# First attention layer of a four-layer graph network: biases of queries and keys as columns at the eviction instead of products with ones

## What is computed

```
q = h @ Wq + bq;  k = h @ Wk + bk;  v = h @ Wv + bv          # layer 0, 12 heads of 32
scores = q k^T / sqrt(32) + beta * adj;  masked where adj is not over 0
x = x + softmax(scores) v
x = x + directed(h; W_left, W_self, W_right, biases)          # layer 1, one pass
x = x + directed(directed(h))                                 # layer 2, two passes
x = x + attention(h; Wq, Wk, Wv, bv, adj as bias) @ Wo.T + bo # layer 3: no bias on q and k
```

## Time and profile before

| what | value |
|---|---|
| median of three runs | 2525.0 us |
| profiled execution: its own time | 2528.0 us |
| profiled execution: span of the core | 2526.3 us |
| mean granted TensorE clock | 0.972 of full speed |
| TensorE busy | 2353.9 us (93%) |
| VectorE busy | 1981.3 us (78%) |
| ScalarE busy | 1778.4 us (70%) |
| GpSimd busy | 1635.4 us (65%) |
| chain that ended last, by engine | TensorE 82%, GpSimd 3%, DMA 2% |

### The profile page before, as it was taken

How to read it: one execution, slowest core, us unless ns; L and a number is a source line. 1 busy time by engine, 2 the same in 40 slices (tenths; PEclk the granted TensorE clock), 3 DMA queues, 4 the chain that set the end, 5 groups by cost and what they waited for, 6 DMA issues and landing times.

```text
span 2526.3 us, 80379 instructions
## 1 busy us (share of the span) xinstructions
PE 2353.9 (93%) x26817; PEld 1741.8 (69%) x26817; DVE 1981.3 (78%) x8945; ACT 1778.4 (70%) x4412; POOL 1635.4 (65%) x2196
## 2 busy tenths in 40 slices
PE   2259999999999999999999999999999999999985
PEld 1146777777777777777777777777777777777753
DVE  4557788888887878888878888878888888888873
ACT  2336777777777777777777777777777777777763
POOL 1026777677766766777677767766777677767762
PEclk8579999999999999999999999999999999999996
DMA  3311333233223332223232323232322223322321
GB/s 102 105 51 39 69 66 70 60 72 63 69 62 66 65 71 58 67 65 73 58 66 65 74 59 68 65 68 62 64 66 71 62 64 66 71 62 64 63 53 35
DMA packets 479851, 165.39 MB, mean 65 GB/s; under 512 B 413392, under 2 KB 479440, under 8 KB 479440
## 3 DMA queue, kind: packets, MB, share of 16 engines
q1 hardware_dynamic: 479440, 160.25, 28.6%
HBM read 46.92 MB, written 12.58 MB: 24 GB/s over the span
## 4 chain that ended last, share of the span: by engine, by line
PE 82%; POOL 3%; issue 3%; DMA 2%; DVE 1%; ACT 0%; SPq 0%; DVEq 0%; POOLq 0%; ACTq 0%
PE bank L148 20%; PE bank L150 20%; PE bank L149 20%; PE bank L1360 4%; PE bank L1298 4%; PE bank L1347 2%; DMA pT<-p 2%; PE bank L1252 1%; PE bank L1314 1%; PE bank L1316 1%; PE bank L1315 1%; PE bank L1405 1%; PE bank L1403 1%; PE bank L1402 1%; POOL p L587 1%
## 5 line engine op out<-in xcount | busy, mean ns | idle before, releaser
L148 PE MATMUL bank<-w_hi,dir_hT_hi 128*128 128x384 f16 x1728 | 564.7, 327 | 0.0
L149 PE MATMUL bank<-w_lo,dir_hT_hi 128*128 128x384 f16 x1728 | 564.3, 327 | 0.0
L150 PE MATMUL bank<-w_hi,dir_hT_lo 128*128 128x384 f16 x1728 | 564.1, 326 | 0.0
L587 POOL TENSOR_TENSOR p<-probs,p 128x512 f16<-128x512 f32 x384 | 447.1, 1164 | 133.8 <-ACT p L699 133.1
L692 ACT ACTIVATE probs<-minus_scores,minus_max 128x128 f32<-128x128 f32 x1536 | 488.1, 394 | 63.1 <-DVE minus_max L909 63.1
L148 PE MATMUL bank<-hT_hi,w_hi 128*128 128x128 f16 x2304 | 412.6, 220 | 0.7 <-DVE hT_lo L895 0.7
L149 PE MATMUL bank<-hT_lo,w_hi 128*128 128x128 f16 x2304 | 412.5, 220 | 0.0
L150 PE MATMUL bank<-hT_hi,w_lo 128*128 128x128 f16 x2304 | 412.4, 220 | 0.0
L909 DVE CUSTOM_DVE_ANT_0 minus_scores<-bank,minus_score_bias 128x128 f32<-128x128 f32 x1536 | 343.5, 286 | 23.7 <-issue 13.4
L595 POOL TENSOR_TENSOR raw_weights<-raw_weights,gain_offset 128x384 f32<-128x384 f32 x192 | 191.9, 999 | 166.4 <-ACT raw_weights L779 166.4
L149 PEld LDWEIGHTS bank<-w_lo,dir_hT_hi 128*128 128x128 f16 x1728 | 169.5, 98 | 112.5 <-issue 1.2
(11 more groups left out here) (164 smaller groups left out, 7250.0 us busy)
## 6 DMA issues: line engine op xcount, KB each, us to landing
x<-in_x SPq DMA_DIRECT2D x64, 192.0 KB, 2.6
dir_adj_tile<-in_adj SPq DMA_DIRECT2D x192, 64.0 KB, 2.1
out<-raw_weights SPq DMA_DIRECT2D x64, 192.0 KB, 2.2
adj_tile<-in_adj SPq DMA_DIRECT2D x128, 64.0 KB, 2.1
pT<-p SPq DMA_TRANSPOSE x384, 2.8
raw_weights<-in_L_gnn_Wq SPq DMA_DIRECT2D x2, 576.0 KB, 4.2
raw_weights<-in_L_gnn_Wk SPq DMA_DIRECT2D x2, 576.0 KB, 5.6
raw_weights<-in_L_gnn_Wv SPq DMA_DIRECT2D x2, 576.0 KB, 6.4
```

The source lines that it names most:

```text
L148: pe.matmul(out, stat[0], move[0], start=first, stop=False)
L149: pe.matmul(out, stat[0], move[1], start=False, stop=False)
L150: return pe.matmul(out, stat[1], move[0], start=False, stop=last)
L587: pool.tensor_tensor(p16[:, c, 1, :, :], probs[:, HC * c:HC * c + HC, :], p16[:, c, 0, :, :], ALU.subtract).then_inc(p_lo[c], 1)
```

## The change

The bias products are taken out of `project_turned`. The q and k biases are loaded as columns, one value per partition, in six small DMAs ahead of the weights; GpSimd makes the scaled negative of the q bias once. The evictions of "first" tasks become three instructions of 128x128 each, with the column of their block as bias; those of "last" tasks stay. The two biases no longer take part in the search for the scales, and their rows are no longer made.

```diff
+        raw_columns, q_bias = sb("raw_q_k_bias_columns", [P, 2, C]), sb("minus_q_bias", [P, C])
+        columns_loaded = sem("q_k_bias_columns_loaded")
...
-        W0 = Weights(names("L0", "Wq", "Wk", "Wv"), names("L0", "bq", "bk"), [([0], [0]), ([1], [1]), ([2], [])], False,
-                     0, 0, 0, 2, 1, [(v_bias[:, :], ins["L0_gnn_bv"]), (raw_beta[:, :], ins["L0_gnn_beta"])])
+        W0 = Weights(names("L0", "Wq", "Wk", "Wv"), [], [([0], []), ([1], []), ([2], [])], False,
+                     0, 0, 0, 0, 2, [(v_bias[:, :], ins["L0_gnn_bv"]), (raw_beta[:, :], ins["L0_gnn_beta"])])
...
+                def load_columns(sp):
+                    for n, name in enumerate(("L0_gnn_bq", "L0_gnn_bk")):
+                        for c in range(C):
+                            sp.dma_start(raw_columns[:, n, c:c + 1], ins[name][c128(c)].rearrange("(p o) -> p o", o=1)).then_inc(columns_loaded, 16)
...
                 load_x(Task(ATTENTION, "first", 0))
+                load_columns(sp)
                 W0.load(sp)
...
                     pool.tensor_scalar(minus_beta[:, :], raw_beta[:, :], -1.0, None, ALU.mult).then_inc(w_kept_by_pool, 1)
+                    pool.wait_ge(columns_loaded, 32 * C)
+                    pool.tensor_scalar(q_bias[:, :], raw_columns[:, 0], -float(HD ** -0.5), None, ALU.mult).then_inc(w_kept_by_pool, 1)
...
-                    n = is_last(t)
-                    act.activation(qT[:, :], q_bank[:, 0:D], ACT.Copy, scale=q_unscale[:, n:n + 1]).then_inc(q_ready, 1)
+                    if is_last(t):
+                        act.activation(qT[:, :], q_bank[:, 0:D], ACT.Copy, scale=q_unscale[:, 1:2]).then_inc(q_ready, 1)
+                        return
+                    for c in range(C):
+                        part = act.activation(qT[:, c128(c)], q_bank[:, c128(c)], ACT.Identity, bias=q_bias[:, c:c + 1],
+                                              scale=q_unscale[:, 0:1])
+                    part.then_inc(q_ready, 1)
...
-                    act.activation(kT[:, :], k_bank[:, 0:D], ACT.Copy, scale=unscale[:, n:n + 1]).then_inc(k_ready, 1)
+                    if is_last(t):
+                        act.activation(kT[:, :], k_bank[:, 0:D], ACT.Copy, scale=unscale[:, n:n + 1]).then_inc(k_ready, 1)
+                        return
+                    for c in range(C):
+                        part = act.activation(kT[:, c128(c)], k_bank[:, c128(c)], ACT.Identity, bias=raw_columns[:, 1, c:c + 1],
+                                              scale=unscale[:, n:n + 1])
+                    part.then_inc(k_ready, 1)
...
-                W0.bias_rows_high(act, bias_rows, [(0, 0, 0), (1, 1, 1)])
                 W0.split_high(act)
...
-                W0.bias_rows_low(dve, bias_rows, [(0, 0, 0), (1, 1, 1)])
                 W0.split_low(dve)
...
                     for m in range(C):
-                        if not is_last(t):
-                            pe.matmul(bank[:, c128(m)], bias_rows[:, w, c128(m)], first_and_33rd[:, :], start=True, stop=False)
                         for c in range(C):
                             mm = three_products(pe, bank[:, c128(m)],
                                                 (weights.w_hi[:, w, c, c128(m)], weights.w_lo[:, w, c, c128(m)]),
-                                                hTs(t, c), first=c == 0 and is_last(t), last=c == C - 1)
+                                                hTs(t, c), first=c == 0, last=c == C - 1)
```

## The result

The changed kernel takes 2505.2 us (median of six runs, 2504.0 to 2508.0) beside 2524.9 us of the kernel before in the same series (six runs, 2523.4 to 2525.5). The ratio is 0.9924, interval 0.9911 to 0.9937: 19.7 us less. Forecast were 2504.3 us, in a range of 2499 to 2510. The profiled execution took 2505.8 us around a span of 2504.0, 22.3 less than the span before.

The account below looks back on a forecast made before the run. TensorE's back-to-back instructions were taken as the bound. Products -21.2 us, evictions nothing and start +0.5 made -20.7: 2528.0 profiled becomes 2507.3, and 3.0 less for the median gives 2504.3 us, range 2499 to 2510.

Parts of the forecast that it names:

- The bound: Middle rounds: TensorE's instructions one behind the other set the pace, 35.96 us for an undisturbed round.
- the six products: First layer's key and query projections, three bias products each: 0.056 us apiece, 0.336 us a graph, 21.2 us over 63 graphs.
- a pair costs more than its pitch: Rival at TensorE's bias products: the 98 ns weight load sets the spacing, so 37 us go, 2488 us; chance 0.03.
- The evictions: First-layer query and key evictions on ScalarE: each 0.6 us longer, 77 us more over 64 graphs, costing nothing in time.
- the cover: Three idle times on ScalarE hide the longer evictions; without it each graph would pay up to 1.2 us.
- 1.38 us of slack, of which 0.6 goes: Between the query eviction's end at 1233.86 and the scores' start at 1235.24; the longer eviction takes 0.6.
- ScalarE becomes the bound: Rival at the query eviction: over 1.38 us late at the scores, +54 us, 2579 us; chance 0.04.
- Transposed probabilities: Rival before the last third of first-layer heads: TensorE's waits take gain back, 3.4 us lost, 2507.7, or 2515; chance 0.08.
- The first graph: Left out of the saving: its longer evictions before the scores eat what the removed products save, so zero.
- The start: Loads, scale search and GpSimd chain before the first round: 0.9 - 1.0 + 0.6 = +0.5 us, bounds -3.5 and +3.5.
- The sum: Whole kernel: -21.2 + 0.5 = -20.7 us, giving 2507.3 us profiled and 2504.3 us as median.
- The rival of no change: A chain once per round without slack takes exactly the removed products' place, so the time stays; chance 0.05.

Follow-up runs that it names:

- The zero products: Changed kernel with six products per graph done again on TensorE with rows of zeros, columns staying on ScalarE: 2523.2 us, ratio 0.9989.
- The six-piece kernel: Changed kernel with query and key evictions of first tasks each cut into six instructions of 128x64 instead of three of 128x128: 2551.7 us, ratio 1.0100.
- the experiment with six pieces of queries: Changed kernel with only the query eviction of first tasks in six instructions of 128x64, the key's staying in three: 2515.8 us, ratio 0.9963.
- both edits: Changed kernel with negations of beta and query bias on VectorE and column loads issued behind the weights: 2501.1 us in second batch, 2497.4 in third.
- the columns behind: Changed kernel with the six column loads issued after the first layer's weights instead of ahead of them: 2501.7 us, ratio 0.9906.

## Why the prediction was right

**The bound and the six products: right.** The period fell by 0.33 us, forecast 0.336, to 35.63, forecast 35.62. The zero products alone bring 0.33 back. The rival by which a pair costs more than its pitch falls with this: removing six pairs from each round moved the period by 0.055 us each. For the 81 ns of the Trainium skill, "TensorE: Matmul & The Clock Gate", section "Back-to-back issue gap", cited in the prediction, this means that the trace did not agree, nor did the runs; 81 would have shown as 0.49 us a round.

**The evictions: right in size and in cost, wrong in the cover.** Each took 0.57 us more, forecast 0.6, one piece 453 to 468 ns, forecast 0.43 to 0.49. ScalarE rose by 70 us, forecast 77, to 74%. The idle time before the queries' eviction went to zero, as worked out. That before the exponent shrank from 0.61 to 0.31 only, where I had said to about zero: the queries' eviction ends 0.57 us later against the scores, but the exponent's operand from VectorE comes later too (0.50 us ahead of the scores instead of 0.77), and the difference of 0.30 is what the idle time lost. The left eviction behind it starts 0.16 us after the scores, 0.17 before, so nothing was handed on. The step that was mis-sized is "1.38 us of slack, of which 0.6 goes": the end of the eviction and the start of the scores are not neighbours at distance zero, for 0.25 us of hand-off belong between them. The real cover was 1.13 before and is 0.56 now. This changed nothing for the forecast, as 0.6 fits in 1.13, but it decides how near the edge the kernel stands: the experiment with six pieces of queries cost 11 us where I had forecast 0 to 5 by the same mistake. The condition of the rival "ScalarE becomes the bound", 1.38 us late, was for the same reason 0.25 too generous. The six-piece kernel shows that rival's mechanism, at 47.4 us, when it is forced.

**Transposed probabilities: right.** They are waited for 8 times and 4.5 us in all (10 and 6.7 before). Not one round in the median lost its gain.

**The first graph: the gain of half a microsecond is not the change's.** I took this graph as zero, because "its longer evictions eat what it saves". From the first product to the scores it is 5.90 us, before 6.40 (34.61 to 41.01). Timeline of TensorE after:

```profile
34.00 0.29 PE L148 MATMUL bank<-hT_hi,w_hi 128*128 128x128 f16 x1 [1.17 <-DVE hT_lo L915]
34.29 0.31 PE L148 MATMUL bank<-hT_hi,w_hi 128*128 128x128 f16 x1
...
37.10 0.22 PE L148 MATMUL bank<-hT_hi,w_hi 128*128 128x128 f16 x1
37.27 0.22 PE L148 MATMUL bank<-hT_hi,w_hi 128*128 128x128 f16 x1
...
39.90 0.95 PE L1315 MATMUL bank<-kT,qT 32*128 32x128 f32 x24 [1.29 <-issue]
```

The products start 0.107 us apart up to 37.05 and 0.056 after it: a slow stretch of 3.0 us from the first product on. In the kernel before it lasts 4.6 us (to 39.17), and in the two other profiled executions of the changed kernel 3.8 and 2.6, so its length moves without any edit. From the first product to the last it is 4.38 us, before 5.46 (34.61 to 40.07), so 1.08 less. 1.5 us less of the slow stretch is worth 0.7 of that by the two spacings, an estimate that leaves some 0.36 for the six products. Two kernels of the first batch show it without an estimate, since the slow stretch lasts 3.81 us in both: the repeated changed kernel and the one with the products back. First and last product of the repeated changed kernel:

```profile
34.19 0.29 PE L148 MATMUL bank<-hT_hi,w_hi 128*128 128x128 f16 x1 [1.18 <-DVE hT_lo L915]
...
38.95 0.22 PE L150 MATMUL bank<-hT_hi,w_lo 128*128 128x128 f16 x1
```

And with the products back:

```profile
33.77 0.29 PE L1279 MATMUL bank<-ones_in_rows_and,bias_rows 128*128 128x128 f16 x1 [1.18 <-DVE hT_lo L916]
...
38.86 0.22 PE L150 MATMUL bank<-hT_hi,w_lo 128*128 128x128 f16 x1
```

4.76 against 5.09 us: the six products are worth 0.33 us in the first graph too, and the longer query eviction costs 0.58 there (1.52 us from the last product to the scores, before 0.94). So the change itself makes the first graph some 0.25 us longer. My zero is near to this, and the half microsecond that the profile shows beside it is chance. The slow stretch is also what the first scores of the start's experiments lost: with the negations on VectorE the slow stretch lasts 4.6 us, with both edits 4.0 in the third batch and in the second until the last product.

The slow stretch looks like the lower level of the clock, which the views do not show: they give a granted clock of 1.00 on both sides of 37.05. But the trace's first record of the clock begins at 37.0 here, at 39.2 in the kernel before and at 38.0 in the repeated changed kernel, just where the spacing changes, and for the time ahead of it there is none. And in the stretch of 1691.20 to 1694.60 above, at a granted clock of 0.50, products of 128x128 start 0.107 us apart as well. TensorE had been idle until the transpositions (31.95) 2 us before the first product.

**The start: wrong in sign, small in size.** Forecast +0.5, bounds -3.5 to +3.5; measured -0.6 at VectorE's first work (-1.1 at the first scores, by the first graph's chance). VectorE's search began 0.4 later, not 0.9: six column loads cost 2.8 us of issue (1.36 + 1.38 for twice three), not 3.2. GpSimd was mis-sized more, in two terms of opposite sign. I left the first negation at its 1.21 us and added 0.6; it took 0.26, and the second 0.23, so two instructions took 0.57 us with the gap between them, where one had taken 1.21. And I took the idle stretch ahead of them as fixed; it went from 7.06 to 7.60 us, and with that ate the half microsecond by which the reduction ended earlier. None of this could be read off the old trace, and the bounds held it. At graph 5 the changed kernel is 0.5 us ahead, not 1.1: the wait of the weights' preparation for a transfer is 1.0 longer (20.3 us, 19.3 before). That wait was 21.5 and 19.6 us in other executions of changed kernels; it moves by 1 to 2 us for reasons that the edits do not explain.

**The sum: right, and in part by luck.** 20.7 us were forecast; the medians of the series differ by 19.7, and 22.3 came off the profiled span. The 58 rounds from graph 5 on gave 19.1, against 58 x 0.336 = 19.5 in the forecast. The five other graphs that I counted, four ahead of graph 5 and the last one, were to give 1.7 more, and no trace shows it. From the first graph's instruction on GpSimd to that of graph 5 it is 267.8 us before and 267.9 after (266.8 and 268.8 in the other two profiled executions of the changed kernel), so 1.3 us would be hidden in what that stretch moves by itself. And the end, with the last graph's projections in it, takes 131.0 us, 130.9 before. The start, forecast 0.5 later and come 0.6 earlier, made up for most of this. The 2.7 us by which the stalls of the two profiled executions differ are chance too: the round of 39.49 us with its fall of the clock alone is 3.5. It fits that this execution of the kernel before stood 3 us above its median, and that the spans differ by more than the medians. The rival of no change had a place to hold, a chain once per round without slack; there was none.

**Open.** What sets GpSimd's idle stretch after the reduction over partitions: 7.06 us before, 7.60, 7.59 and 7.18 in the changed kernel, 9.90 with the columns behind, 8.34 and 8.24 with both edits. Whether the order of the two waits matters in the changed kernel itself, where the slack of 0.56 should hide it, wasn't tried alone; the kernel without key bias has the other order and the same period. And what decides when the first graph's products turn from 0.107 to 0.056 us.

## What to carry to other kernels

On an engine that is full in every round, the price of a removed instruction is its distance to the next start in that very stretch: 0.056 us in this kernel, never the 0.22 us of a row. Before a gain in the first microseconds is put down to an edit, compare how long the slow spacing lasted in both executions, and repeat the profile: here it moved the first scores by more than six products did. A single round that is several microseconds over the median, with a fall of the clock in it, makes one profile a poor measure of the stalls. Before trusting slack, take the hand-off off it, and look for stalls between starts rather than in idle time, since matmul tails cover short ones. When several semaphores stand ahead of a critical instruction, wait for the one that comes last in last place, and ask of every bias whether the next step removes it anyway.

## What the runs showed of the hardware that was not expected

- From ScalarE's last write to TensorE's first matmul that reads it: 0.25 us with another, satisfied wait behind the late one, 0.15 us with the late one last. It is worth 0.13 us a round where the slack is used up (35.82 to 35.69).
- The same negation of 128x1 on GpSimd took 1.21 us in the kernel before and 0.26 us in the changed ones, at the same place behind a long idle stretch.
- Small ScalarE instructions out of PSUM start closer than they last: three of 128x128, 453 to 468 ns each, take 1.15 us; six of 128x64 take 1.88, so half the columns save little.
- Loads of a few bytes per partition cost their issue: three took 1.36 us on the queue, and with all six behind the weights VectorE's start moved 3.5 us forward.
- In the first graph, products of 128x128 start 0.107 us apart for 2.6 to 5.5 us from the first one on, and 0.056 after that. The changed kernel alone shows 3.0, 3.8 and 2.6 us in three executions, while the view has the granted clock at 1.00 all through.
- One wait of 1.74 us in the middle of a full run was followed by 3.4 us at a granted clock of 0.50, and that round took 3.5 us more than the median.
